# Values of half a sequence stacked on 128 partitions and turned by two full transpositions

## The reference

```
b, s, _ = h.shape                      # 2, 1024
q = (h @ wq).reshape(b, s, 32, 64)     # 32 heads of 64 channels
k = (h @ wk).reshape(b, s, 8, 64)      # 8 groups, 4 heads of q to each
v = (h @ wv).reshape(b, s, 8, 64)
scores = q . k / sqrt(64), causal
attn = softmax(scores)
out = (attn @ v) @ wo
```

## Time and profile before

| | us |
|---|---|
| median of 3 runs (lowest to highest) | 1832.38 (1832.23 to 1833.19) |
| profiled execution, span from the first to the last instruction | 1831.4 |
| its TensorE busy | 1742.7 |
| its VectorE busy | 1036.2 |
| its ScalarE busy | 1059.7 |
| its GpSimd busy | 207.9 |

### The profile page before, as it was taken

How to read it: one execution, slowest core, us unless ns; L and a number is a source line. 1 busy time by engine, 2 the same in 40 slices (tenths; PEclk the granted TensorE clock), 3 DMA queues, 4 the chain that set the end, 5 groups by cost and what they waited for, 6 DMA issues and landing times.

```text
span 1831.4 us, 31651 instructions
## 1 busy us (share of the span) xinstructions
PE 1742.7 (95%) x12158; PEld 1387.1 (76%) x12158; DVE 1036.2 (57%) x2595; ACT 1059.7 (58%) x2376; POOL 207.9 (11%) x236
## 2 busy tenths in 40 slices
PE   7999799999999999999999999999939999999993
PEld 6777477777777777777777777777739999999993
DVE  3777667777677677686686677676661111111112
ACT  3344677777777787787777787777731222222223
POOL 2223100000000000000000000000011222222222
PEclk9999899999999999999999999999968999999997
DMA  3000100000000000000000000000053153113533
GB/s 87 1 2 2 47 1 10 1 1 10 1 1 10 1 1 10 1 1 10 1 1 10 1 1 1 1 1 24 1 193 112 23 160 92 29 23 92 153 102 97
DMA packets 46102, 60.17 MB, mean 33 GB/s; under 512 B 8993, under 2 KB 39585, under 8 KB 45985
## 3 DMA queue, kind: packets, MB, share of 16 engines
q1 hardware_dynamic: 35088, 46.15, 7.5%
q0 software_dynamic: 7536, 10.36, 3.4%
q10 hardware_dynamic: 3360, 2.10, 0.4%
HBM read 138.43 MB, written 11.40 MB: 82 GB/s over the span
## 4 chain that ended last, share of the span: by engine, by line
PE 93%; DVE 3%; ACT 1%; POOL 1%; DMA 1%; issue 1%; ACTq 0%; POOLq 0%; DVEq 0%
PE wide L1441 15%; PE bank L1355 14%; PE bank L1343 14%; PE wide L1326 9%; PE bank L1292 9%; PE wide L1327 8%; PE bank L1450 7%; PE bank L1364 6%; PE bank L1153 3%; PE wide L1165 1%; PE bank L1239 1%; PE bank L1178 1%; PE bank L1228 1%; PE bank L1282 1%; PE bank L1126 1%
## 5 line engine op out<-in xcount | busy, mean ns | idle before, releaser
L921 DVE CUSTOM_DVE_ANT_0 arena<-wide,arena 128x896 f32<-128x896 f32 (+7 forms) x512 | 382.9, 755 | 249.3 <-PE wide L1327 243.1
L671 ACT ACTIVATE arena<-arena,nmax 128x896 f32<-128x896 f32 (+7 forms) x512 | 399.1, 780 | 90.0 <-DVE nmax L921 87.8
L683 ACT COPY arena<-bank 128x512 f32<-128x512 f32 x576 | 311.5, 586 | 82.7 <-PE bank L1343 77.1
L1326 PE MATMUL wide<-khi,qhl 128*128 128x512 f32 (+3 forms) x768 | 345.2, 450 | 1.4 <-DVE vt L905 1.3
L1343 PE MATMUL bank<-ident,arena 128*128 128x128 f32 x2304 | 309.4, 274 | 1.7 <-DVE arena L929 0.5
L1441 PEld LDWEIGHTS wide<-wo,arena 128*128 128x128 f32 x2496 | 286.9, 193 | 3.3 <-issue 1.4
L1441 PE MATMUL wide<-wo,arena 128*128 128x128 f32 x2496 | 287.3, 276 | 1.0 <-ACT wo L727 1.0
L1343 PEld LDWEIGHTS bank<-ident,arena 128*128 128x128 f32 x2304 | 260.0, 141 | 28.6 <-issue 13.4
L1355 PE MATMUL bank<-arena,vt 128*64 128x256 f32 x2304 | 276.9, 385 | 0.0
L929 DVE TENSOR_SCALAR arena<-arena,rinv 128x896 f32<-128x896 f32 (+7 forms) x512 | 257.8, 525 | 9.1
L1085 DVE TENSOR_TENSOR wo<-wide,wo 128x512 f32<-128x512 f32 x78 | 53.9, 691 | 368.2 <-PE wide L1441 368.2
(11 more groups left out here) (232 smaller groups left out, 1569.3 us busy)
## 6 DMA issues: line engine op xcount, KB each, us to landing
arena<-in_L_ffn_w SPq DMA_DIRECT2D x117, 1024.0 KB
wq_g<-in_L_ffn_wq SPq DMA_DIRECT2D x8, 256.0 KB, 3.0
wo<-in_L_ffn_wo SPq DMA_DIRECT2D x16, 128.0 KB, 3.1
hbuf<-acc SPq DMA_DIRECT2D x2, 1024.0 KB, 4.5
tbuf<-rT_all SPq DMA_DIRECT2D x4, 512.0 KB, 3.0
acc<-hbuf SPq DMA_DIRECT2D x4, 512.0 KB, 5.9
out<-x_all SPq DMA_DIRECT2D x8, 256.0 KB, 2.1
x_all<-in_L_attn_x ACTq DMA_DIRECT2D x2, 896.0 KB, 9.1
```

What stands on the lines that cost most here:

```text
L671: nc.scalar.activation(probs[t % 2][:, h, 0:w], probs[t % 2][:, h, 0:w], ACT.Exp, bias=nmax[:, t % 2, h:h + 1], scale=-1.0, accum_out=rsum ...
L683: nc.scalar.copy(pT[t % 2][m], bank_of((t, m))).then_inc(S("pT_ready"), 1)
L921: nc.vector.tensor_tensor_reduce(out=probs[t % 2][:, h, 0:w], in0=score_bank(t, h)[:, 0:w], in1=causal[:, SEQ - w:SEQ], scale=-1.0, scalar ...
L1326: mm(dst, q, khi[:, lo:lo + cols], start=True, stop=False)
```

## The change

`vT` holds the same values on 128 partitions: token blocks 0 and 1 of a half on partitions 0 to 63 and blocks 2 and 3 on partitions 64 to 127. ScalarE writes it by two copies of 64 x 256 in place of one of 64 x 512. Item V becomes two transpositions of 128 x 128, each of which gives one block of the lower partitions and one of the upper in 128 columns. VectorE's copy has the same size and puts the blocks, which stand in the order 0, 2, 1, 3, back in theirs.

```diff
-        vT = sb("vT", [DH, SEQ])
+        vT = sb("vT", [P, SEQ // 2])
@@ ScalarE, evacuate(item)
-                    nc.scalar.copy(vT[:, half * HALF:(half + 1) * HALF], src[DH:P]).then_inc(S("vT_ready"), 1)
+                    for j in range(2):
+                        ins = nc.scalar.copy(vT[j * DH:(j + 1) * DH, half * 2 * P:(half + 1) * 2 * P], src[DH:P, j * 2 * P:(j + 1) * 2 * P])
+                    ins.then_inc(S("vT_ready"), 1)
@@ VectorE, low_part(item)
-                    nc.vector.tensor_copy(vt[:, n % 2, half * TB // 2:(half + 1) * TB // 2], src[:, 0:TB // 2 * DH].rearrange("p (t d) -> p t d", d=DH)).then_inc(S("v2_ready"), 1)
+                    nc.vector.tensor_copy(vt[:, n % 2, half * TB // 2:(half + 1) * TB // 2].rearrange("p (j x) d -> p j x d", j=2),
+                                          src[:, 0:2 * P].rearrange("p (x j d) -> p j x d", x=2, j=2)).then_inc(S("v2_ready"), 1)
@@ TensorE, project(item)
-                    for x in range(TB // 2):
-                        cols = (half * TB // 2 + x) * P
-                        ins = nc.tensor.transpose(to[:, x * DH:(x + 1) * DH], vT[:, cols:cols + P], ident[0:DH, 0:DH])
+                    for x in range(2):
+                        cols = (half * 2 + x) * P
+                        ins = nc.tensor.transpose(to[:, x * P:(x + 1) * P], vT[:, cols:cols + P], ident[:])
```

## The result

The changed kernel takes 1827.61 us (median of 6 runs, 1825.54 to 1830.01), the kernel before, in the runs beside them, 1832.79 us. The ratio is 0.9971, with a 95% interval from 0.9961 to 0.9981, so the gain is small but clear of the noise: 5.2 us, where 4.5 were forecast (median 1827.9).

The account below looks back on a forecast made before the run. TensorE was taken to bound the kernel, carrying 93% of the chain of waits. Span 1831.4 - 4.5 = 1826.9 us, plus 1.0 around it, gave a median of 1827.9 us; range 1825.5 to 1831.4.

Parts of the forecast that it names:

- What an item costs, before and after: TensorE's transpositions of one half's values: 0.59 us before, 0.22 us with two full ones, saving 0.37 us.
- V2 pays nothing: Second-half item: its 0.37 us goes into TensorE's wait at ct = 4 for VectorE's normalised probabilities, 0.17 growing to 0.54 us.
- V1 pays nearly all: First-half item: 0.30 us of 0.37 kept, 15 x 0.30 = 4.5 us.
- the wait for the bank: First-half transpositions wait until a copy frees their PSUM bank: 0.06 to 0.07 us lost.
- item H0: Another TensorE item, starting 0.08 us after a copy's end; its four matmuls take 1.38 us where others take 1.32.
- ScalarE's copies cost nothing: Two half copies on ScalarE take 0.16 us more at most, covered by 2.17 us of idle time.
- VectorE's copy: VectorE's copy to `vt`, 0.42 us, same element count in another order; costed at nothing even if doubled.
- The clock: TensorE's granted clock in the loop: under 1.00 would show the forecast wrong.
- all 31 items pay: Rival: VectorE's chain behind the second-half item moves with TensorE, 11.5 us saved, 1820.9 us; 5 in 100.
- the columns count: Rival: border gaps stay, a first-half item saves only 0.08 us, 1.2 us in all, 1831.2 us; 15 in 100.
- V1's gain is absorbed: Rival: later normalised heads swallow part or all of the 4.5 us, at worst 1832.4 us; 10 in 100.
- the clock drops: Rival: the longer 0.54 us wait lowers TensorE's clock once a sequence, costing 30 us, 1857.9 us; 3 in 100.

Follow-up runs that it names:

- four_full: Changed kernel with each of the two full transpositions issued twice, so 4 x 128 columns: 70.54 us a sequence, single run 1832.73 us.
- v2_only: Kernel before with full transpositions only for the second halves: 1832.54 us against 1832.44, ratio 0.9998.
- short_after: Changed kernel, VectorE normalising only the first 128 of 512 columns per head in one step: 69.80 us a sequence, 1817.22 us.
- short_before: Kernel before, VectorE normalising only the first 128 of 512 columns per head in one step: 70.50 us a sequence, 1828.83 us.
- v1_only: Kernel before with full transpositions only for the first halves: 1827.37 us against 1832.44, ratio 0.9971.
- nf2: Changed kernel, VectorE normalising heads 2 and 3 ahead of the maximum of head 0 in step ct = 2: 1828.93 us, ratio to before 0.9972.
- act_only: Kernel before with only ScalarE's copy of the values split into two of 64 x 256, old layout: 70.69 us a sequence, 1835.32 us.

## Why the prediction was right, step by step

**What an item costs, before and after:** right. 0.59 us before and 0.22 now (0.37 less at V2); four_full shows that it isn't the columns that count. One reading was loose: the old transpositions don't all start 0.06 us apart. In the trace of before the second starts 0.11 us behind the first, and only the two behind it at 0.06.

**V2 pays nothing:** right, and for the reason given. A sequence of v2_only is within 0.01 us of before, its wait at ct = 4 is 0.64 us, and short_after and short_before show that it is VectorE's work that ends this wait.

**V1 pays nearly all:** right in kind, and 0.05 us off in size. The mis-sized term is the wait for the bank, which I took from item H0 as 0.06 to 0.07 us; it is 0.02. So V1 saves 0.35 us and not 0.30, 15 x 0.35 = 5.2 us, which is what the medians show, and a sequence takes 70.35 us and not 70.40. That the forecast median of 1827.9 lies within 0.3 us of the measured 1827.6 is in part luck: the saving is off by 0.7 us, and the kernel before took 1832.8 us beside it, 0.4 more than the 1832.4 that the sum started from. The bank is free equally soon in both places (the copy ends 0.08 us ahead of the recorded start). What differs is the weight load that follows: TensorE's loads (PEld) in the changed kernel start at 259.88 for V1, about 0.05 us behind the end of the copy, and for H0 likewise:

```profile
259.88 0.20 PEld L1285 LDWEIGHTS bank<-ident,vT 128*128 128x128 f32 x2
...
409.32 0.30 PEld L1295 LDWEIGHTS bank<-rT_all,wkv_g 128*128 128x128 f32 x2
```

By their source lines a load for L1295 lasts 0.19 us and one for L1285 0.14; that difference of 0.05 would be just the difference of the two waits. This reading was not tested by a run of its own.

**ScalarE's copies cost nothing:** right in the end. But "0.16 more at most" was wrong: it is 0.29 (0.77 less the 0.48 from the old copy to the exponential). I took two copies by their durations and forgot that the old copy, 0.58 us long, overlapped its follower by 0.1 us. The new ones don't overlap theirs. Against 2.17 us of cover it didn't matter.

**VectorE's copy:** 0.42 us as before, right. **The clock:** 1.00 from 214 to 1270 us, right; the wait of 0.54 us beyond the shortest distance, once in a sequence, didn't lower it.

**The rivals:** that all 31 items pay is excluded by v2_only, that the columns count by four_full, that V1's gain is absorbed by v1_only, and that the clock drops by the granted clock of 1.00.

## What to carry to other kernels

An engine that the profile shows as busy for 99.9% of a loop, like TensorE here, may still not pass on what it saves: look for the next place at which it waits, and ask of the work that ends this wait whether it hangs on an instruction behind the saving (then it moves too) or ahead of it (then it stays, and swallows the gain). Transpositions whose shape differed from their neighbours' cost more here (0.59 us for four) than the same number with twice the columns in their neighbours' shape, so compare start times over the whole group, not durations. And when one wait is removed by reordering, the next one in the queue must be removed with it: nf2 gained nothing, and together with the oT copy 0.28 us a sequence.

## What the runs showed of the hardware

- A group of four 64-row transpositions among 128-row instructions costs 0.59 us, though its second starts 0.11 us behind the first and the last two 0.06 us apart. Four 128-row transpositions with twice the columns make a sequence 0.16 us shorter (four_full).
- Two copies of 64 x 256 on ScalarE, each 0.37 us long, take 0.54 us to the start of the follower in act_only, where both write partitions 0 to 63, and 0.77 us in the changed kernel, where the second writes partitions 64 to 127. In the first case each starts its follower after 0.27 us, in the second after 0.38 and 0.39, so neither overlaps it. In both kernels the copies read the same PSUM partitions, 64 to 127; they differ in where they write, and I had not expected that to matter. No run takes the reason apart.
- VectorE's copy out of PSUM with its blocks of 64 elements permuted takes the same 0.42 us as in order.
